# Seven half steps spread among thirty-two whole steps in the routed part of a transformer block

## What is computed

```python
xn = _layernorm(x)
# attention: out = softmax(QK^T)V + xn ; normalized = (out - mean) / sqrt(var + 1e-8)
#            return gamma * normalized + beta
shared_out = (silu(xf @ sw1) * (xf @ sw3)) @ sw2
g = einsum('td,edh->teh', xf, w1);  u = einsum('td,edh->teh', xf, w3)
moe_out = einsum('te,teh,ehd->td', cw, silu(g) * u, w2)     # two experts of 8 per token
return x + attention(xn) + moe_out + shared_out
```

## Time and profile before

| what | us |
|---|---|
| median of 3 runs (1849.96 to 1851.47) | 1851.2 |
| the profiled execution | 1853.11 |
| its span | 1851.3 |
| PE busy in the span | 1708.6 |
| POOL busy | 1178.7 |
| ACT busy | 1091.7 |

### The profile page before, as it was taken

The page is one execution under the profiler, slowest core; times in us unless marked ns, Lnnn a source line. Parts: engine busy times, 40 slices in busy tenths (PEclk is TensorE's granted clock), DMA queues, the critical chain, the costliest instruction groups (busy, mean ns, idle before and its releaser), DMA issues.

```text
span 1851.3 us, 35725 instructions
## 1 busy us (share of the span) xinstructions
PE 1708.6 (92%) x12066; PEld 1287.0 (70%) x12066; DVE 1267.1 (68%) x3089; ACT 1091.7 (59%) x2072; POOL 1178.7 (64%) x1441
## 2 busy tenths in 40 slices
PE   3489999998999899999799999999999999999998
PEld 2255555555555555554488888888888888888887
DVE  6888888888888888877544554455455454566666
ACT  5247567666676566766556666666666666333332
POOL 4466557776677667846257777777777787553443
PEclk9689999999999999999899999999999999999999
DMA  1444445444445454454655766756667675465543
GB/s 54 154 127 122 129 128 173 154 156 157 144 150 162 141 171 150 159 171 172 221 189 180 237 191 201 232 192 212 216 197 222 200 229 188 149 188 149 158 146 99
DMA packets 246374, 313.29 MB, mean 169 GB/s; under 512 B 31546, under 2 KB 210884, under 8 KB 240068
## 3 DMA queue, kind: packets, MB, share of 16 engines
q1 hardware_dynamic: 233924, 277.60, 47.3%
q0 software_dynamic: 12288, 33.57, 5.7%
HBM read 211.70 MB, written 98.86 MB: 168 GB/s over the span
## 4 chain that ended last, share of the span: by engine, by line
PE 47%; ACT 1%; DMA 1%; DVE 1%; POOL 1%; issue 0%; SPq 0%; DVEq 0%; ACTq 0%
PE gu L2006 29%; PE yp L2020 15%; PE xt L1995 2%; DMA early_raw<-in_L_ffn_w_dram 0%; DVE hf L1876 0%; DMA early_raw<-in_L_ffn_sw_dram 0%; ACT early_high L1771 0%; ACT sil L1777 0%; ACT hid_h L1779 0%; POOL early_low L1679 0%; POOL early_down L1679 0%; POOL w_up_l L1679 0%; POOL rows L1740 0%; DVE hid_l L1879 0%; ACT xc L1785 0%
## 5 line engine op out<-in xcount | busy, mean ns | idle before, releaser
L650 ACT ACTIVATE pT<-st_ps 128x512 f32<-128x512 f32 x682 | 368.6, 563 | 265.7 <-PE st_ps L1305 258.9
L923 DVE CUSTOM_DVE_ANT_0 s_ps<-s_ps,masks 128x384 f32<-128x384 f32 (+1 forms) x512 | 314.6, 633 | 39.6 <-PE s_ps L1284 34.1
L2006 PE MATMUL gu<-xc,early_high 128*128 128x512 f32 (+1 forms) x1120 | 337.9, 385 | 2.5 <-DVE xc L1887 1.5
L1876 DVE TENSOR_TENSOR hf<-sil,gu 128x512 f32<-128x512 f32 (+1 forms) x220 | 143.7, 653 | 275.9 <-ACT sil L1777 275.9
L1284 PE MATMUL s_ps<-k_aug,q_aug 97*128 97x512 bf16 (+3 forms) x1024 | 262.2, 309 | 37.9 <-DVE mx L923 23.4
L1303 PE MATMUL st_ps<-q_aug,k_aug 99*128 99x512 bf16 (+1 forms) x992 | 268.9, 303 | 11.8 <-ACT pT L650 6.7
L1879 DVE TENSOR_TENSOR hid_l<-hf,hid_h 128x512 fp32r<-128x512 f32 (+1 forms) x220 | 175.1, 796 | 147.7 <-ACT hid_h L1779 147.7
L2006 PEld LDWEIGHTS gu<-xc,early_high 128*128 128x128 f32 x1120 | 205.4, 190 | 44.4 <-POOL early_low L1679 4.0
L1779 ACT ACTIVATE hid_h<-hf 128x512 fp32r<-128x512 f32 (+1 forms) x220 | 133.1, 605 | 174.2 <-DVE hf L1876 174.2
L1777 ACT ACTIVATE sil<-gu 128x512 f32<-128x512 f32 (+1 forms) x220 | 123.9, 563 | 180.5 <-PE gu L2006 180.5
L2006 PE MATMUL gu<-xc,early_low 128*128 128x512 f32 (+1 forms) x560 | 214.3, 383 | 0.0
(11 more groups left out here) (260 smaller groups left out, 3889.5 us busy)
## 6 DMA issues: line engine op xcount, KB each, us to landing
w_raw<-in_L_ffn_w_dram SPq DMA_DIRECT2D x60, 512.0 KB, 6.5
early_raw<-in_L_ffn_w_dram SPq DMA_DIRECT2D x57, 512.0 KB, 5.7
part_scr<-parts SPq DMA_DIRECT2D x64, 384.0 KB, 3.8
q_aug<-part_scr SPq DMA_DIRECT2D x192, 128.0 KB
k_aug<-part_scr SPq DMA_DIRECT2D x192, 128.0 KB
early_raw<-expert_rows SPq DMA_DIRECT2D x34, 512.0 KB
expert_results<-yo SPq DMA_DIRECT2D x32, 512.0 KB, 3.3
x_sb<-in_L_attn_x_dram SPq DMA_DIRECT2D x16, 512.0 KB, 4.1
```

The source lines that it names most:

```text
L650: fn(pT[j][:, h:h + heads], unit_view(column_bank(b, u), heads, w), ACT.Exp).then_inc(exp_done, 1)
L923: vec.tensor_tensor_reduce(bank[:, 0:keys], bank[:, 0:keys], masks[:, 2 * C + P - keys:2 * C + P], 1.0, LOWEST, ALU.add, ALU.max, mx[:, h ...
L1876: vec.tensor_tensor(hf[:, m % 2, 0:w], sil[:, m % 2, 0:w], gu[m % 2][:, 1, 0:w], ALU.mult).then_inc(h_done, 1)
L2006: last = mm(gu[m % 2][:, a, 0:width(n)], w_up[wpar][x][:, a, c, P * m:P * (m + 1)], xc[par][:, y, c, 0:width(n)], start=k == 0, stop=k == ...
```

## The change

Every fifth routed step, 5, 10, up to 35, is now a half step; the other 32 of the 39 are whole. `chunk_of(n)` maps a step to the same chunk of rows as before, so each step's work is what it was. Sixteen second norms need sixteen even steps: all even ones from 2 to 38 but 10, 20 and 30. The half steps 5, 15, 25 and 35 are odd and still hold a `norm_end` and a `load_norm`; there POOL now does `norm_end` behind all six pieces instead of behind two. The last norm's store has moved to the first shared step. The routed steps are written out on all engines; before, ACT, DVE, POOL and SP had a loop over pairs of steps.

```diff
+        SPACING = WHOLE // HALVES + 1
+        NO_NORM = tuple(n for n in range(SPACING, CHUNKS + 1, SPACING) if n % 2 == 0)
+        NORM_AT = {n: k + 1 for k, n in enumerate(n for n in range(2, CHUNKS, 2) if n not in NO_NORM)}
+        def half_step(n):
+            return 0 < n <= CHUNKS and n % SPACING == 0
         def width(n):
-            return S // 2 if known(n) and WHOLE < n <= CHUNKS else S
+            return S // 2 if half_step(n) else S
+        def chunk_of(n):
+            return WHOLE + n // SPACING if half_step(n) else n - n // SPACING
-        def routed(engine, step, written_out=False):
-            for n in range(1, 5):
-                step(n, n % 2, (n + 1) // 2, 1 if n >= 3 else None)
-            if written_out:
-                for n in range(5, 2 * B + 1):
-                    step(n, n % 2, (n + 1) // 2, (n - 1) // 2)
-            else:
-                with engine.Fori(2, B) as pair:
-                    for odd in range(2):
-                        step(pair * 2 + odd + 1, 1 - odd, pair + 1, pair)
-            for n in range(WHOLE + 1, CHUNKS + 1):
-                step(n, n % 2, None, B if n < WHOLE + 3 else None)
+        def routed(step):
+            for n in range(1, CHUNKS + 1):
+                step(n, n % 2, NORM_AT.get(n + n % 2), NORM_AT.get(n - 2 + n % 2))
...
                 if c == 1:
                     store_result(CHUNKS)
+                    store_norm(B)
...
                 cut_low(n + 1, 1 - par, (0, 1))
-                if par == 1 and ends is not None:
+                if par == 1 and ends is not None and not half_step(n):
                     norm_end(ends)
                 if par == 0 and begins is not None:
                     norm_root(begins)
                 cut_low(n + 1, 1 - par, range(2, PIECES))
+                if par == 1 and ends is not None and half_step(n):
+                    norm_end(ends)
```

More of the change, by code:

```diff
@@ L1502, in known @@
             return isinstance(v, int)
+        SPACING = WHOLE // HALVES + 1
+        NO_NORM = tuple(n for n in range(SPACING, CHUNKS + 1, SPACING) if n % 2 == 0)
+        NORM_AT = {n: k + 1 for k, n in enumerate(n for n in range(2, CHUNKS, 2) if n not in NO_NORM)}
+        assert CHUNKS // SPACING == HALVES and len(NORM_AT) == B and NORM_AT[CHUNKS - 1] == B
+        def half_step(n):
+            return 0 < n <= CHUNKS and n % SPACING == 0
         def width(n):
[L1506 removed]
+            return S // 2 if half_step(n) else S
+        def chunk_of(n):
+            return WHOLE + n // SPACING if half_step(n) else n - n // SPACING
         def piece(q, par):
             return weight_piece(q, w_raw[par], w_up[par], w_dn[par])
[L1512 to L1529 removed]
+        def routed(step):
+            for n in range(1, CHUNKS + 1):
+                step(n, n % 2, NORM_AT.get(n + n % 2), NORM_AT.get(n - 2 + n % 2))
         def shared(step):
@@ L1554, in load_routed @@
             def load_routed(k, par):
-                sp.reg_load(expert_reg, plan["expert"][0:1, bass.ds(k - 1, 1)])
+                sp.reg_load(expert_reg, plan["expert"][0:1, bass.ds(chunk_of(k) - 1, 1)])
                 e = sp.snap(expert_reg)
@@ L1560, in chunk_rows @@
             def chunk_rows(n):
-                sp.reg_load(row_reg, plan["row"][0:1, bass.ds(n - 1, 1)])
+                sp.reg_load(row_reg, plan["row"][0:1, bass.ds(chunk_of(n) - 1, 1)])
                 row = sp.snap(row_reg)
@@ L1603, in store_result @@
                     return
-                first = WHOLE * S + (n - 1 - WHOLE) * S // 2 if width(n) < S else (n - 1) * S
+                r = chunk_of(n) - 1
+                first = WHOLE * S + (r - WHOLE) * S // 2 if half_step(n) else r * S
                 sp.dma_start(expert_results[bass.ds(first, width(n)), :].rearrange("(t p) c -> p t c", p=P),
@@ L1659, in _ @@
             load_routed(2, 0)
-            routed(sp, routed_step)
+            routed(routed_step)
             shared(shared_step)
@@ L1756, in _ @@
             pool.wait_ge(params_in, 32)
-            routed(pool, step)
+            routed(step)
             pool.wait_ge(y_stored, 16 * (CHUNKS + 1))
@@ L1862, in _ @@
             first_step()
-            routed(act, routed_step)
+            routed(routed_step)
             shared(shared_step)
@@ L1974, in _ @@
             first_step()
-            routed(dve, routed_step)
+            routed(routed_step)
             shared(shared_step)
@@ L2054, in _ @@
             routed_step(0, 0, None, None)
-            routed(pe, routed_step, written_out=True)
+            routed(routed_step)
             shared(shared_step)
```

## The result

The changed kernel takes 1878.0 us in the median of four runs (1876.6 to 1880.0), the kernel before 1850.9 in four runs: 1.0148 times as long, with an interval of 1.0134 to 1.0162. The prediction was 1875.0, slower by 24.0; it is slower by 27.1.

A forecast was written before the change was run, and what follows sets the result against it. PE was taken to bound the kernel, so only its pauses could be won or lost: -8.55 + 11.3 + 18.8 + 2.4 = +24.0 us on the median of 1851.2, which gives 1875 us, range 1861 to 1886.

The forecast's parts named there:

- What is removed: PE's pauses at steps 33, 34 and 39 to 40, in the row of half steps, all go: -8.55 us.
- The borders: At each of seven half steps PE waits 1.19 ahead of `down` and 0.43 ahead of the next tile: 11.3 us.
- The norm behind a half step: In steps 6, 16, 26 and 36 the norm's rows land late and PE waits: 4.7 us each, 18.8 in all.
- The wait of 0.95 ahead of `up(7, 0)`: Behind step 6, PE waits 0.95 us more for POOL's two pieces after `norm_root`; likewise at the other three places.
- The clock: Behind the pause of tile 3 in steps 6, 16, 26 and 36, PE runs slower: 0.6 us each, 2.4 in all.
- Costed at nothing: Written-out loops and the last norm's store, moved behind `store_result(39)` in step 40, were taken to cost no time.
- the norm is in time: Rival: the late `norm_sum` has cover, so only borders count: +2.8 us, 1854 us; chance 0.08.
- the border is covered too: Rival: no wait at `down(n - 1)` in half steps and the norm in time: -5.5 us, 1846 us; chance 0.06.
- The slip is carried on: Rival: late step 8 weights or step 7 `norm_end` cost each of four places 2 to 3 us more: 1883 to 1887; chance 0.12.

The follow-up runs named there:

- e6: The kernel before with its routed steps written out on ACT, DVE, POOL and SP too, order unchanged: 1851.68 us, ratio 1.0012.
- f3: The kernel before with SP loading the shared expert's weights in half step 38 ahead of the store of the result: 1845.65 us, ratio 0.9973.
- e2: The changed kernel with PE taking tile 1 ahead of `down` in half steps: 1876.87 us, ratio 1.0147 to the kernel before.
- f2: The changed kernel with tile 1 of half steps ahead of `down` on PE and ahead of ACT's wait for it, copy behind tile 2: 1876.78 us, ratio 1.0146.
- e3: The changed kernel with SP loading the rows of step 42 first in the first shared step: 1875.06 us, ratio 1.0135 to the kernel before.
- e1: The changed kernel with a second pair of norm buffers, its two loads not waiting for `norm_end` and first in SP's odd step: 1870.8 us, ratio 1.0107.
- f1: The changed kernel with the norm's sum, squares and root moved later within steps 6, 16, 26 and 36: 1875.27 us, ratio 1.0134 to the kernel before.
- g1: The changed kernel with the edits of e1, f2 and e3 together: 1853.17 us, ratio 1.0015 to the kernel before.
- e7: The changed kernel with its half steps in a row at 31 to 37, norms at 2 to 30 and 38: 1854.75 us, ratio 1.0027 to the kernel before.
- e4: The changed kernel with `norm_end` of half steps 5, 15, 25 and 35 back behind two pieces: 1874.07 us, ratio 1.0124 to the kernel before.

## Why the prediction was right, point by point

Sizes from the profiled executions (PE's steps), against the predicted terms:

| term | predicted | measured |
|---|---|---|
| pauses removed | -8.55 | 111.5 - 7 x 9.73 - 2 x 17.60 = 8.2, so -8.2 |
| seven borders | 11.3 | 7 x (16.27 + 15.57 + 14.80 - 2 x 17.69 - 9.73) = 7 x 1.53 = 10.7 |
| four norms behind a half step, clock included | 18.8 + 2.4 = 21.2 | 4.65 + 4.74 + 5.05 + (5.90 + 0.89) = 21.2 |
| 40 to 41 | 0 | 20.13 - 17.54 = 2.6 |
| whole steps, written out | 0 | 26 x 0.09 in e6 = 2.3; about 2 here |
| 19 to 20 | 0 | 16.64 - 16.28 = 0.4 |
| steps 0 to 3, and around the expert phase | 0 | -0.9, and -1.8 |
| sum | +24.0 | +26, the spans' difference; the medians differ by 27.1 |

The last four terms were not foreseen; they are +5.0 and -2.7, so that in the sum they half cancel.

**What is removed** held: nothing waits at step 39, and the same pause could be had without the change (f3).

**The borders** held, in cause and size. The wait that the profile gives to POOL is DVE's `hid_l`, which ends 0.10 ahead of `down(4)`, POOL's last piece 0.67 ahead of it. With a tile put between, the wait went (e2), and with ACT's order fitted, 1.87 came back at every border (f2), more than the 1.62 that I counted, since the wait of 0.2 to 0.3 that even a steady half step has went as well.

**The norm behind a half step** held as a chain: issue, landing (5.0 against 4.9), sums, squares, copy, tile. That the sum of 21.2 agrees to a tenth is luck: the terms lay otherwise within it. The wait of tile 3 was predicted at 3.7 and was 2.86 to 3.27, since `norm_sum` took 2.39 and `norm_end` ended 0.2 earlier. The wait of 0.95 ahead of `up(7, 0)` did not come in after, because tile 3 took 1.5 to 2.5 longer at half clock and POOL's pieces were ready behind it. It is there where the clock stayed up. Steps 6 and 26 of e3 and step 26 of e2 have such a pause with a granted clock of 1.00 behind it. PE of e3, step 26:

```profile
1370.97 0.73 PE L2015 MATMUL gu<-xc,early_high 128*128 128x512 f32 x2 [2.82 <-DVE hf L1885]
...
1375.17 0.73 PE L2015 MATMUL gu<-xc,w_up_h 128*128 128x512 f32 x2 [1.17 <-POOL w_up_l L1686]
```

The tile takes 3.03 and the wait behind it 1.17. In those three places the step is 16.4 long without its pause, 1.6 above 14.80. With 12.1 for the four pauses of after, the norms without the clock come to 4 x 1.64 + 12.1 = 18.7, against 18.8 predicted: pauses 2.7 smaller than 4 x 3.7, the rest 2.6 larger than 4 x 1.0.

**The clock** came out at its size by luck too. "I take 0.6, near the row" rested on one row at step 40, where the rate came back early, and was to come four times. The steps of after without their pause are 16.59, 16.49, 16.58 and 17.76 long, against 16.44 where the clock stayed up (e2, e3). So the fall added about 0.1 in each of the first three, since the wait ahead of `up(7, 0)` would have been there anyway, and 1.3 in the fourth; with the 0.9 from 37 to 38, which I count to it without having shown it, that is 2.5 where 2.4 was predicted. The Trainium skill says in "TensorE: Matmul & The Clock Gate", part 1, that throttled is the default and that activity releases it. The trace agrees in that the granted clock is 0.50 behind each of the four pauses and comes back as PE goes on. That all of the tile would run at half rate was my own step from there, and it does not hold: 5.48 would be the whole tile, and three of the four took 4.21 to 4.45.

**What e1 took from it.** I had the four places as the landing's work. They are the landing's only in the order of this kernel: with the rows in time (e1) 2.5 stays, with the work moved behind the landing (f1) the pause comes a step later, and a border covered without the rows in time gives nothing (f2). What stays in g1, 2.8 a place, is in part three pauses of PE, in step 6 0.30 ahead of `down(5)`, 0.62 (released by `hf`) and 1.14 (by POOL's `w_up_l`). The cause is POOL, I think: from 1002.9 to 1023.1 of that trace it has one gap, of 0.57, with a piece, `norm_beta`, six pieces, `norm_end`, `norm_sum` and two pieces in a row, and its wait for the squares comes only then. That POOL's own work is what remains is argued from this, not shown by an experiment.

**Costed at nothing** failed twice. "The loads behind it are first used two steps on" was wrong for step 40: the rows behind the store are transposed in the very next step, and it cost 2.6 (e3). "Register operations between waits would only be fewer" was wrong too: DVE's `hf` began later, and the whole steps took 0.07 to 0.09 more (e6). The trace before could have told it: its own written-out steps took 17.68, those of the loop 17.60 to 17.65.

**The rivals.** Neither "the norm is in time" nor "the border is covered too" came; e1 and f2 made each of them, and g1 both at once: 1853.2. The rivals had 1854 for the norm in time alone and 1846 for both; neither had POOL's own work or the cost of writing out in it. The 1853.2 also has the 2.6 of step 40 taken out, which the rivals cost at nothing. "The slip is carried on" came at one place of four (18.58 from 37 to 38, 0.9 us), not at all of them.

## What to carry to other kernels

A short step among long ones loses cover on both sides: list for each engine what was hidden behind the long step's tile and what work of fixed length (here a norm's load and POOL's part of it) does not shrink with the step. Where two waits end close together, taking away one shows little (e1 gave 7 us back and f2 1, both with e3's 2.6 gave 25), so their removal is to be tried together before either is given up. And before work is reordered to hide a late load, look at where the load stands in its queue: one load moved ahead of one store gave more than all of the reordering.

## What the runs showed of the hardware that was not expected

DVE's `hid_l`, with both inputs in SBUF, takes 0.42 us for a half tile, but 1.67 and 1.70 where POOL has an operation of 2.57 in flight, and ends 0.28 behind it. The same happens after, beside `norm_end`, which ends at 1018.64:

```profile
1017.25 1.67 DVE L1887 TENSOR_TENSOR hid_l<-hf,hid_h 128x256 fp32r<-128x256 f32 x1 [0.48 <-ACT hid_h L1787]
...
1019.74 0.42 DVE L1887 TENSOR_TENSOR hid_l<-hf,hid_h 128x256 fp32r<-128x256 f32 x1 [0.48 <-ACT hid_h L1787]
```

It was there before the change, too: 22 of the 28 half tiles in the trace before took 0.52 to 1.32 and ended 0.28 behind an operation of POOL, weight pieces among them. `hf`, which has one input in PSUM, keeps its 0.41 to 0.42 in e1 beside the same work of POOL. The Trainium skill says so in "SBUF — State Buffer", "Who interferes with whom": a VectorE instruction with two SBUF inputs contends with a GpSimd instruction that reads SBUF. The trace agrees, and it counts the wait as DVE's busy time, not as idle time, so no view of waits shows it.

Whether a pause of PE costs clock is not told by its length alone in these runs. The granted clock was 0.50 to 0.53 for a stretch of the work behind the four pauses of 2.86 to 3.27 us in after, and also fell behind pauses of 1.99 (e1), 2.31 (e7), 2.32 (e4) and 2.79 us (e3, step 16). It stayed at 1.00 behind 2.43 (after, step 41), 2.81 and 2.82 (f1, four times), 2.82 and 3.14 us (e3, steps 26 and 6). Behind those of 1.02 and 0.37 us at the borders it stayed at 1.00 every time. From 41 to 42 this alone made 17.6 or 19.1 us of the same work. And writing loops out made whole steps longer, by 0.07 to 0.09 each (e6), where I had thought that fewer operations could only help.
